# Remade order tables: longer runs of attention-score steps on TensorE

## The reference, cut to what matters

```
x = x + 0.5 * ffn0(ln(x));  x = x + attn0(ln(x));  x = x + 0.5 * ffn0(ln(x))     # layer 0
x = x + 0.5 * ffn1(ln(x));  x = x + attn1(ln(x));  x = x + 0.5 * ffn1(ln(x))     # layer 1
ffn0: (silu(y Wg.T) * (y Wu.T)) Wd.T, weights (int - 128) * scale per row, hidden width 704
ffn1: (sigmoid(y W1.T) * (y W2.T)) W3.T, weights clip(round(w / mean|w|), -1, 1)
attn0: 16 heads of 16, rotary, causal softmax(q k / 4) v, output projection
attn1: 16 query heads on 4 key/value heads, ALiBi bias, causal softmax, projection plus bias
```

## Time and profile before

| | |
|---|---|
| median of three runs | 648.75 us |
| the profiled execution | 647.0 us, of which the span from first to last instruction is 645.2 |
| TensorE matmuls busy | 578.3 us (90%), 5770 matmuls |
| VectorE busy | 477.6 us (74%), 806 instructions |
| ScalarE busy | 405.6 us (63%), 644 instructions |
| GpSimd busy | 253.2 us (39%), 279 instructions |
| TensorE's mean granted clock | 0.974 of full speed |

### The profile page before, as it was taken

One profiled execution on the slowest core, in us unless ns is written; L12 is line 12 of the kernel. 1 busy time (PEld: TensorE's weight loads), 2 busy tenths in 40 slices (PEclk: granted clock), 3 DMA queues, 4 the chain that ended last, 5 costly groups with the idle time before them and its releaser, 6 DMA issues.

```text
span 645.2 us, 14201 instructions
## 1 busy us (share of the span) xinstructions
PE 578.3 (90%) x5770; PEld 314.8 (49%) x5770; DVE 477.6 (74%) x806; ACT 405.6 (63%) x644; POOL 253.2 (39%) x279
## 2 busy tenths in 40 slices
PE   2798985888969998999999999999998997999986
PEld 1355542544533553556545465556554543555553
DVE  4789899987797779785867776886866676763442
ACT  5846645357765486665866756675857657767542
POOL 7674777320153327225223541335244012032433
PEclk9989999889988999999999999999999899999999
DMA  9500033231143013401230103010301141101200
GB/s 341 237 1 2 1 49 61 39 50 38 37 68 66 2 36 62 75 9 26 50 60 10 36 9 74 18 21 18 62 1 36 21 79 37 36 35 34 71 35 33
DMA packets 18577, 31.84 MB, mean 49 GB/s; under 512 B 6176, under 2 KB 7584, under 8 KB 18232
## 3 DMA queue, kind: packets, MB, share of 16 engines
q1 hardware_dynamic: 18512, 30.94, 20.5%
HBM read 13.75 MB, written 2.36 MB: 25 GB/s over the span
## 4 chain that ended last, share of the span: by engine, by line
PE 45%; DVE 13%; DMA 10%; POOL 9%; ACT 8%; issue 8%; SPq 5%; POOLq 0%; DVEq 0%; ACTq 0%
PE PS L518 11%; PE PS L547 8%; PE PS L637 7%; DMA RB<-scratch 5%; PE PS L597 4%; PE PS L619 3%; DVE MX L941 3%; POOL HH L1018 3%; ACT PB L767 3%; SPq L433 2%; PE PS L469 2%; DMA scratch<-DC 2%; PE PS L652 2%; PE PS L496 2%; POOL OC L1046 2%
## 5 line engine op out<-in xcount | busy, mean ns | idle before, releaser
L767 ACT ACTIVATE PB<-PS 128x1024 f32<-128x1024 f32 x160 | 160.3, 1018 | 61.9 <-PE PS L469 61.0
L941 DVE TENSOR_REDUCE MX<-PS 128x2 f32<-128x1024 f32 (+2 forms) x192 | 158.4, 862 | 47.1 <-PE PS L469 46.8
L518 PE MATMUL PS<-XT,WGU 128*128 128x512 f16 x640 | 160.1, 391 | 3.6 <-DVE XT L872 1.7
L1018 POOL TENSOR_TENSOR HH<-TH,HH 128x512 f16<-128x512 f32 (+1 forms) x96 | 104.7, 1098 | 147.8 <-ACT HH L726 147.6
L518 PEld LDWEIGHTS PS<-XT,WGU 128*128 128x128 f16 x640 | 56.3, 99 | 73.2 <-issue 10.6
L469 PE MATMUL PS<-MASKM,MASKW 64*128 64x128 bf16 (+1 forms) x1280 | 83.0, 207 | 0.0
L547 PE MATMUL PS<-WD,HH 128*128 128x256 f16 x640 | 78.2, 276 | 2.9 <-POOL HH L1018 2.5
L637 PE MATMUL PS<-PB,V 128*32 128x512 f32 (+3 forms) x1024 | 76.4, 439 | 2.2 <-ACT PB L767 2.2
L597 PE MATMUL PS<-SK,SQ 54*128 54x256 f16 (+3 forms) x512 | 63.5, 307 | 13.0 <-DVE TH L891 3.7
L726 ACT ACTIVATE HH<-TH 128x512 f16<-128x512 f32 (+1 forms) x96 | 55.3, 589 | 29.9 <-PE PS L547 10.5
L619 PE MATMUL PS<-SQ,SK 55*128 55x384 f16 (+3 forms) x512 | 62.6, 303 | 10.4 <-ACT PB L767 4.1
(11 more groups left out here) (92 smaller groups left out, 750.3 us busy)
## 6 DMA issues: line engine op xcount, KB each, us to landing
SQ<-QPB SPq DMA_DIRECT2D x48, 128.0 KB, 4.2
OC<-OT SPq DMA_DIRECT2D x64, 64.0 KB, 2.3
RB<-scratch SPq DMA_DIRECT2D x32, 128.0 KB
SK<-QPB SPq DMA_DIRECT2D x24, 128.0 KB, 4.7
out<-X SPq DMA_DIRECT2D x4, 512.0 KB, 2.8
PB<-wd SPq DMA_DIRECT2D x2, 768.0 KB, 10.7
PB<-gu SPq DMA_DIRECT2D x2, 704.0 KB, 6.0
PB<-gu SPq DMA_DIRECT2D x1, 1408.0 KB, 12.0
```

The source lines that it names most:

```text
L518: m = e.matmul(o[:, :], WGU[l][:, k, col:col + P], XT[0][j][:, k, :], start=first, stop=last)
L767: e.activation(PB[Q % 2][:, j, :, :], two_banks("s", i), ACT.Exp, scale=0.25).then_inc(a_exp, 1)
L941: e.tensor_reduce(MX[:, Q % 4, :, pr, t], o[:, :, col:col + (t + 1) * P], AX.X, ALU.max, negate=True).then_inc(a_max, 1)
L1018: e.tensor_tensor(HH[1][:, s * T:s * T + wd], TH[:, i % 3, 0:wd], HH[0][:, s * T:s * T + wd], ALU.subtract).then_inc(f_lo, 1)
```

## The change

All six tables are made anew and nothing else. Each engine's new string has every letter as often as the old one, so the same steps run with the same instructions; only their order on each engine and the banks differ. On TensorE the score steps stand in longer runs: before, 173 of the 220 visits were of a single step; after, 33 of 134. In the opening `a` stands 18th and not 39th, and the last `z` stands behind the last FFN's last `G`.

```diff
--- before.py
+++ after.py
@@ -94,44 +94,44 @@
...
     "sp":
-        "kkkrrkrDrSRrDSrRrkDSRkrrDSrRkrkDSrRrlDSRrkkrDSrRrlDSRrkkrDSRrrDSRrkkrDSrRrDSrRkkrDSRrrDSrRrOrDSRDSOR"
...
+        "kkrrkrDkSrRrDSRrrkDrkSRrDSRrkrDSkrRrlDSRrkkrrDSRlrDrSkRkrDrSRrDSrRkrkrDSRrDSRrrkkDrSROrDSrRrDSrRDSRO"
...
     "pe":
-        "ttggGGgGgzGgGgGttggGGddddgGzgGgGgGttuuaggGGddgGgGddgGzgGqqvvttddddqggqGuuGgGgGgGzqqgGmmmmmdmdmdmxqmq"
-        "sdsmsmsmsxmpsmsmsmsmxsmmpssmsmxsmsmmmspsxsmsmsmsmpsvmvsxmsmsmuuspmqsqmsmoosxmoosqmspmqsmttggGGsgGsgs"
-        "GzxgmGgmGpmsmsmdsdmdsdmxsmmmpvsvsxsuumtstmqsqmgsGmgsGpmqsxmqsgmGsgmGsgpmGsgmGsomxsomosomspmsmszdmdst"
-        "tmxddsmggGGgGgGzgGgGpsvmvsmuddddsxmusmsmspmqsqmqsxmosomsmttmpsgsGmgsGmxsgmGsgmGsgmGsgmGsomxsompszdmd"
-        "sdmdsttmpsggGGgGgzGgGgGmxvsmuusmddddsqmqsqmpsmosxomtstmmpggGGsgzGsgmGsgmGsgmGsxmomomdsdsdsdmptstmxsm"
-        "mpggGGgzGgGgGsgGsvumuooddddsxmqsqmqsmoosttmpsmggGGgGzgGgGgGsxmtsmtddddsmsmpsmgsGxgmGsgmsmGspmsmsmsmx"
-        "gsmGmspsvmsmuusxgGmsqmqsqmpsmsmsxomsmoompssomsgmGsxmsmpsmsmsmsxtmsmtmpsvsmsggmxsGGmsmspmsgmGszxmdsdm"
-        "dsdmgsGmgsGmososxspzgsGsosospsddpttddggGGgzGgGgGgGooooddddttggGGgzGgGgGgGdddd",
+        "ttGggGGGggggGGttzagggddddGGgggGGuuGGqvvqtztqgGqGggddddgGGggGGzttmmmumdmmudxgGmgqmdsqmsGGmsgdxsqmsgmm"
+        "spmssqsmmsgxpmmGssGsmsgmszGxpmmdmsdmsmdssdxsmmmmpsvvsmmsmxuusmsmqqpssmosoooxssmmqqpmsttmsssmgGgxGgGg"
+        "GgGgGzssmmmmddddmsspsmsxmmmpsvvssmsuuxmttsmqqmsmspoooomssqqxgGmsmgGgGmsmpsggsmGGsxgGszttpmmgdmdssmdm"
+        "ssdxmGmsggGmspmvvGuusmsgGgxsmsqGgmmsqGqoooommzsddxddssmmpssmsmmssttxpsmsgGGGgggGssmgGgGmttsmspzmmmdd"
+        "xmddssgGgGssmpmvgxuuGmsgqqqmsmGgssGgmmspxGmoooomzsmddddsmspmsmssxmmttpsgGggGGgGmsmgGssmgxGsmttmzsddd"
+        "pgvmsmdgGxGssmgGgsmgGmspuumsGgmmGoqoqqooxzssmdmsmdssddmsssmxppmmmttssmgGgGgGxgsmsGgGsmsgGmsmpsvtzmsd"
+        "msmdddxmmmpsstxoooossGgGGuugggqqqmmsGgGmmspsmsgGxssmtmtzsddddmsmpmsmssxgmmmpsvssmssmxgmmmpssGmgmsxmG"
+        "ssmgsooossosspmmpGxGgGsssgsGsttzpGgGgggggddddGGGGoooozddddttGgGGgggGGggGzdddd",
     "dve":
-        "NwNttshshsshhwwNsshhttNsshhwdwwdswhnsshhswhttwwsshhdsuhuwdsshnhpsqhrpwqwrdttdpsqnrphqsrhusuhsshphqps"
-        "qrrhmmmmmmmmdpmqprqdrmmnmmmmmmmmmmcmmmmmmmmCmcmmmuumCpqmropmqorNpmqprqcrttmmsshhmshshmsChsmhmmmdmdmN"
...
+        "NwNttshshwwswhwwswhsshhwtwtwswdwdwnhNsshhuusNphqsprqhrttshpsqhrpqsshrddhnsshhshmtmmmtmmuumdsspmqhrmh"
+        "pmqsrhdmpmmqmrnmpmqsrmhmcsmhmshmmmdmCmdmmmmncmmmuummCppqqrrmooNpmqmrmpmttqmrsshhcshshshshmmmmdCdmNmm"
...
     "act":
-        "wwXxxwXttwhhttwwhhtwxxtwwhhXtwtwhhtthttYxxhhhyyttXthhhttthqhqYhQxxvvQqttqyyQhYQthtthqhqthQQhnqqeeeQe"
...
+        "wwXwxxwXttwhhtwwhtxtxtwhwhhwwttthYtyhyhXttqvvhqxxQXQhqthqQttQhhhttthhxYxhyynttqeqeQethneQqethehoeeQe"
...
     "pool":
-        "wwwwwwwwwrwwrhhwwhhrwhhwrdhhdhehhhdhhhdheshhsqdqdsesqhqhhhsshqqhdssqdqeccsqsqrssqqchhhhhhddrcssqhqhs"
...
+        "wwwwwwwwwwwrrwwhhhhwhwhddehrhhrshsqqhshqsdqdhhhehhhdsqshqdshhqesqhhhcddecssqqrsqsqhhhhhhcddrcssqqrhs"
...
     "banks":
-        "0123452436523014523014526701456740151675167450236745236760170452361740236026026026706206202426270640"
-        "2462060462046240264026405260462046270647206420164250462056425640656442454501645062740126720162062062"
...
+        "0123456701230456271045167235041306406407627321014516720644074046010476461460146046560426052605260256"
+        "7024604620562046724624264264206420326402645206403264027460240623240326046032456732670142604640640264"
...
```

More of the change, by code:

```diff
@@ L108 @@
-    "dve":
-        "NwNttshshsshhwwNsshhttNsshhwdwwdswhnsshhswhttwwsshhdsuhuwdsshnhpsqhrpwqwrdttdpsqnrphqsrhusuhsshphqps"
-        "qrrhmmmmmmmmdpmqprqdrmmnmmmmmmmmmmcmmmmmmmmCmcmmmuumCpqmropmqorNpmqprqcrttmmsshhmshshmsChsmhmmmdmdmN"
[L111 to L114, removed]
@@ L115 @@
-    "act":
-        "wwXxxwXttwhhttwwhhtwxxtwwhhXtwtwhhtthttYxxhhhyyttXthhhttthqhqYhQxxvvQqttqyyQhYQthtthqhqthQQhnqqeeeQe"
[L117 to L121, removed]
+        "ttGggGGGggggGGttzagggddddGGgggGGuuGGqvvqtztqgGqGggddddgGGggGGzttmmmumdmmudxgGmgqmdsqmsGGmsgdxsqmsgmm"
@@ new lines @@
+        "msmdddxmmmpsstxoooossGgGGuugggqqqmmsGgGmmspsmsgGxssmtmtzsddddmsmpmsmssxgmmmpsvssmssmxgmmmpssGmgmsxmG"
+        "ssmgsooossosspmmpGxGgGsssgsGsttzpGgGgggggddddGGGGoooozddddttGgGGgggGGggGzdddd",
+    "dve":
+        "NwNttshshwwswhwwswhsshhwtwtwswdwdwnhNsshhuusNphqsprqhrttshpsqhrpqsshrddhnsshhshmtmmmtmmuumdsspmqhrmh"
+        "pmqsrhdmpmmqmrnmpmqsrmhmcsmhmshmmmdmCmdmmmmncmmmuummCppqqrrmooNpmqmrmpmttqmrsshhcshshshshmmmmdCdmNmm"
+        "mmcmumuttmpCqpmqmrroomNhmmhppqhrqmrmcmhhhttmmsmCdmmdmhmnsshmmhcuumshsmhlmsCmhlloommddmNmmmmNttmchhhh"
+        "mhhmttmCmmmmddnshshmmsuuhmcsllmmhslhmmsChmoommddmNmmNmttmchhhhmmhmChmmttdsmmdchsnhmsmhsmhsmuhCummsoh"
+        "lllommmddmNmNmmttmcmhhhmhhCmmhmtmcmmddmmmCnotoNhuuhhllmmhlhmmmchmmttddmCmmmmmmmcmmmmhmmmChmooNmmchhh"
+        "tthChchddhChhhooNddtthhhhhhdd",
@@ new lines @@
+    "act":
+        "wwXwxxwXttwhhtwwhtxtxtwhwhhwwttthYtyhyhXttqvvhqxxQXQhqthqQttQhhhttthhxYxhyynttqeqeQethneQqethehoeeQe"
+        "qetnYoQeeheetehnhoeceeeneoevveenyyeYecqqoeeeQQneeqqXoeQxxeeettQnhththththeheceeoeneXoevveeyynexxeqcq"
+        "eeoQQeeqqntehtXthehQoetQteenthehxxhotceeeenethteYohvvyyhetetneeQhctehQQheneeoeeXeexnxeoeXtehtththeet"
+        "hthcxxeehonetetheheYotyynvehtQQQeteehtehconheeeoeeXnexxXotehtthhtehtcehtnehexxeotvetnheethteYethohyy"
+        "ecthQQhQneeeeeeeenoXoxxeeXtththnhteehtceethehoevxeencoenexeYteyythththQQXeQthehoeetnehexxeceoeeentoe"
+        "veeeentoeehtenceeteheeeeoXonhhteeeeexxtchohttthhcthththhXxxthtththhtthh",
@@ L122 @@
     "pool":
-        "wwwwwwwwwrwwrhhwwhhrwhhwrdhhdhehhhdhhhdheshhsqdqdsesqhqhhhsshqqhdssqdqeccsqsqrssqqchhhhhhddrcssqhqhs"
-        "sqhqhhhcrehbhhhhhddcrhhhchhhrebhhhhchhddrhhhchhhrebhhhhchhddrrhhhhhhebhhchhhcrhcchhhhhhrchhhchhhrhhh"
+        "wwwwwwwwwwwrrwwhhhhwhwhddehrhhrshsqqhshqsdqdhhhehhhdsqshqdshhqesqhhhcddecssqqrsqsqhhhhhhcddrcssqqrhs"
+        "shhqqhhhchebhhchhhddrrhhhchhhehhbhhchhddrrhhhchhhhehcbhhhhddrrhhhchhhcerbhhhhhhcchhrhhchhchhhhhhrhhh"
         "hhh",
     "banks":
-        "0123452436523014523014526701456740151675167450236745236760170452361740236026026026706206202426270640"
@@ L134 @@
-        "4023640264056204562034602406214062146046021406120461204160216206102323456451023454671012342367012",
+        "0123456701230456271045167235041306406407627321014516720644074046010476461460146046560426052605260256"
+        "7024604620562046724624264264206420326402645206403264027460240623240326046032456732670142604640640264"
+        "0364206104260452634065420640102641012364023674026076407624506210460560460460412601426504236704267014"
+        "2610426052435602460462046024604672304267014523604236706742064206206201456204652301462540162406247024"
@@ L135 @@
+        "6123423604264206420460276405764576204632046320621042610460467012460234610462314602463014253602402402"
+        "4026045426054262546701024603246025460256450264624624062145062104567106745206423064206432064036204624"
+        "0624026740264702460423640264302643026403623406420632454062416024562103245410325046103254676541052",
 }
```

## The result

The kernel after takes 623.24 us (median of 619.60, 622.13, 624.34 and 624.99), the one before 647.93 us over its four runs. The ratio is 0.9596, interval 0.9564 to 0.9627: about 25 us faster, where 13.7 were forecast. The time lies 0.8 us under the range. The profiled execution took 624.34 us, its span 622.6; the profiled one before took 647.0.

What follows compares the result with a forecast made beforehand. From about 206 us TensorE's own list of steps was taken as the bound, before that the opening's chain. Terms -16.2 - 0.5 + 3.5 + 0 - 0.5 = -13.7 gave 633.3 us profiled, 635 us median; range 624 to 647 us.

Steps and rivals of the forecast that it cites:

- Step 1: TensorE: 182 fewer changes of array shape at 0.095 us; 16.2 us gained late, 0.5 us early.
- Step 5: End of the kernel: the last `z` moves into TensorE's wait for the last hidden chunk; 0.5 us gained.
- step 4: Opening: earlier `a` and first attention, third attention about as before; taken as 0, bounds -5 to +3 us.
- Step 2: Longer visits of score steps: evacuations of one kind queue behind each other; 3.5 us lost.
- more than forecast: Rival: waits fall too, more FFN work lies beside the last two attentions; 5 us more, 628 or less; chance 0.12.
- Step 3: Queues behind, with attention's detour through SP's queue: still covered by TensorE work, 13.3 us after; no cost, no gain.

Runs made afterwards that it cites:

- d_one: Kernel after, with the fifth of ten matmuls in each down step `d` issued as two 128 x 64 halves, no step moved: 630.54 us.
- a_split: Kernel after, with 28 visits of two or three score steps broken up in TensorE's table alone: 632.33 us.
- b_merge: Kernel before, with 45 pairs of neighbouring visits joined in TensorE's table alone, from the third attention on: 644.31 us.
- w_late: Kernel after, with VectorE's thirteen weight pieces and TensorE's `a` put back behind their old neighbours: 634.58 us.
- h_end: Spliced tables: the order of the kernel before for steps starting before 400 us, then the order of the kernel after: 638.42 us.
- a_fix: Kernel after, with two neighbours of SP's table exchanged, so the fourth attention's second broadcast goes ahead of a stacking: 618.36 us.
- d_all: Kernel after, with all ten matmuls of each down step `d` issued as two 128 x 64 halves: 625.89 us.
- fin3: All six tables made once more by a search, starting from a_fix; 17 more changes of shape than the kernel after: 604.79 us.
- h_rest: Spliced tables: the order of the kernel before for steps starting before 160 us, then the order of the kernel after: 629.81 us.

## Why the prediction was wrong

Right, by its steps:

- Step 1, the changes of shape, was right in mechanism and size on TensorE's list: 16.5 us in the ledger, 16.7 forecast; the count was certain, and what had to be tested is the price. The same prices held in each rewritten table, and d_one shows them with nothing else changed. The rule of the Trainium skill on changes of tiling mode ("TensorEngine Tiling (Array Packing)", Key Properties) holds here: 128 x 64 against 128 x 128 costs as much as a change of rows does.
- Step 5, the last `z`: 0.6 us less waiting there, 0.5 forecast.
- In step 4 the times of `a` and of the first down steps came true.

Wrong:

- Two steps failed: step 4, by the most, and step 2. Step 2 said "I take 3.5 us lost". Waits for the evacuation of scores fell, from 10.6 to 6.9 us after 206 us. The bound "nothing, or 2 us gained, if only the reuse distance counts" was the right end, and the argument by averages of visits was the wrong one: the 0.28 us a visit that the forecast read off 8 visits of three came out at 0.06 us (2.5 us in all) over the 41 that the new tables have from the third attention on. The old eight stood in tables made for visits of one, which may be why. a_split and b_merge show what a visit's neighbours on the other engines are worth: 6 to 7.5 us of waiting for 28 and 45 moved steps. The rule of the Trainium skill that TensorE's tiling doesn't help evacuation ("Trainium Kernel Development and Optimization", Best Practices) was no argument for a loss here: with longer visits the waits for evacuation fell in sum (10.6 to 6.9 us).
- Step 4, the opening, was taken as 0 with bounds -5 to +3. The third attention's first `m` comes 6.3 us earlier, outside the bounds; two splices give some 7 us, the ledger 9.1, of which 3.1 are clock. I summed VectorE's work up to the third attention and found it equal, which says nothing of what stands ahead of what. The trace had rows for it: the weight pieces between two rotations around 80 us, shown with w_late.
- The rival "more than forecast" named the end of the kernel with 5 us; the ledger has 5.5 us less waiting there, and h_end repeats it. Its place was right and it got a chance of 0.12.
- Step 3, "no cost, no gain", overlooked one entry of SP's table: 4.2 us lost at 369 us, 4.9 us regained by a_fix. It compared the TensorE work that covers the detour and never priced the detour. In that attention 20.0 us lay between the last `p` and the first `o`, well over the 13.3 of the forecast, but the detour took 24.3.

Terms of the difference to the forecast, by the ledger: opening -9.1; end -6.6 (-7.1, of which 0.5 was forecast); middle +9.3, with the 4.2 us of the broadcast and 4.9 of clock, some 3 of which follow that wait; -3.5 for the loss that was forecast and didn't come; +0.8 for the later first matmul. With +0.2 from step 1 they sum to -8.9, and the ledger's -22.7 is 9.0 below -13.7. About 2 us of what is between the profile (-22.7 at the last `d`) and the medians (-24.7) is scatter.

That the total came so near the range (0.8 us under it) is in part luck: the unforeseen gain of the opening and of the end was partly taken back by the unforeseen loss of the middle.

What stays open: why the end waits less. h_end shows that it lies in the order after 400 us, and from the seventh attention on no visit after loses more than 1.1 us by the ledger, where the one of seven in the earlier trace rows lost 3.4, but I have no run that changes only that. And how much of the 16.5 us of step prices reached the time can't be given as one number: b_merge let through 40%, d_one, in the other direction, 50%; in the change itself the rest of the tables was fitted, and losses fell at the same time.

## What to carry to other kernels

Count the changes of the array's shape in TensorE's order and price one from start-to-start times of equal steps; grouping steps of one shape is worth it, above all together with the other engines' orders: regrouped on TensorE alone (b_merge), three fifths of it came back as waits. When all queues are reordered, don't cost the opening and the DMA queue at nothing because their sums are unchanged: look at what stands ahead of each entry on which a long chain hangs. Six large transfers issued ahead of the one that a chain waits for cost that chain their whole issue time here, and the clock's fall behind the wait came on top.

## What the runs showed of the hardware

- Going over between two shapes of the array costs TensorE 0.08 to 0.11 us at either border, whichever two of 64 x 128, 128 x 64, 128 x 32 and 128 x 128 meet: from start to start a gate step takes 0.86 us ahead of its own shape and 0.96 ahead of any other, a `d` 1.09 and 1.19, the widest score steps 0.34 and 0.43, a `p` 2.18 and 2.29. A single pair of 128 x 64 halves between 128 x 128 matmuls costs 0.23 us for both borders. Two halves side by side start 3 ns apart and take together what one full matmul takes (1.09 us for ten, d_all).
- With six stacking transfers issued ahead of it and six behind, the broadcast of two transfers of 128 KB had landed 9.0 us after its issue (361.87 to 370.92 us); with all twelve behind it, it was there at most 8.0 us after (360.56 to 368.56), when the engine first asked for it. Each of these transfers keeps SP's queue for about 0.6 us.
- The granted clock was at the 1.2 GHz level for about 34 us of the span before and 35 after, and in fin3, which waits least, for some 14 us. Behind the projection's wait of 4.2 us in the kernel after such a stretch of 6.8 us stands; a_split, h_rest, w_late and d_one have the wait too (3.1 to 4.8 us) and a stretch of 3.4 to 6.8 us at it, a_fix has neither. d_all has the wait (3.1 us) without a stretch.
